# Graph attention and soft expert layer on one core: the order of work in the first stage

## The reference

```python
x = _layernorm(x)
h = (x @ W1.T).reshape(n, 8, 128)
a_src = jnp.einsum('nhc,hc->nh', h, att_src1)
a_dst = jnp.einsum('nhc,hc->nh', h, att_dst1)
e = leaky_relu(a_src[src] + a_dst[dst], 0.2)
ex = jnp.exp(e - segment_max(e, dst)[dst])
alpha = ex / (segment_sum(ex, dst)[dst] + 1e-16)
out = segment_sum(alpha[:, :, None] * h[src], dst) + b1
```

## Time and profile before

| | |
|---|---|
| median of 3 runs | 1894.87 us (1894.81 to 1895.03) |
| the profiled execution: time, span | 1895.43 us, 1893.6 us |
| busy over the span: PE, DVE, ACT, POOL | 91%, 59%, 45%, 14% |
| mean granted TensorE clock | 0.974 |
| products begin, counting begins, counting ends | 31.8 us, 119.3 us, 366.3 us |
| counting: PE's matmuls of edges | 1062, busy 210.1 us |

### The profile page before, as it was taken

One profiled execution on the slowest core, in us unless ns is written; L12 is line 12 of the kernel. 1 busy time (PEld: TensorE's weight loads), 2 busy tenths in 40 slices (PEclk: granted clock), 3 DMA queues, 4 the chain that ended last, 5 costly groups with the idle time before them and its releaser, 6 DMA issues. The chain is left out here.

```text
span 1893.6 us, 30144 instructions
## 1 busy us (share of the span) xinstructions
PE 1720.6 (91%) x9905; PEld 999.8 (53%) x9905; DVE 1118.7 (59%) x1768; ACT 859.8 (45%) x1358; POOL 266.1 (14%) x116
## 2 busy tenths in 40 slices
PE   3988999689999989889997899999999968998899
PEld 2444444366655646545553555556565645665555
DVE  7998777589999936332231355555555555655311
ACT  2257888688888827311111333333333325555200
POOL 1000000178878614000000000000000000000000
PEclk9999999989999989999999999999999988999899
DMA  6000000002222240110000112221111124330421
GB/s 239 23 1 0 29 0 1 0 25 33 35 46 33 21 147 1 55 62 34 34 26 24 62 67 73 71 72 68 65 65 65 65 73 158 111 109 29 151 67 48
DMA packets 49619, 108.41 MB, mean 57 GB/s; under 512 B 16526, under 2 KB 18664, under 8 KB 49420
## 3 DMA queue, kind: packets, MB, share of 16 engines
q1 hardware_dynamic: 49484, 107.38, 18.5%
q10 hardware_dynamic: 64, 0.08, 0.0%
HBM read 79.02 MB, written 28.43 MB: 57 GB/s over the span
## 5 line engine op out<-in xcount | busy, mean ns | idle before, releaser
L829 POOL TENSOR_TENSOR base<-s_row,ln_c 128x1250 f32<-128x1250 f32 x80 | 227.5, 2846 | 56.1 <-DVE top L884 55.2
L728 PE MATMUL fs<-one_src,one_dst 128*128 x1062 | 210.1, 342 | 25.5 <-ACT one_dst L656 14.6
L93 PE MATMUL di_l<-x2t_hi,ph_hi 128*128 128x512 f16 (+1 forms) x576 | 196.3, 341 | 12.4 <-DVE ph_lo L1471 11.0
L94 PE MATMUL di_l<-x2t_lo,ph_hi 128*128 128x512 f16 (+1 forms) x576 | 196.2, 341 | 0.0
L95 PE MATMUL di_l<-x2t_hi,ph_lo 128*128 128x512 f16 (+1 forms) x576 | 196.1, 340 | 0.0
L588 DVE TENSOR_SCALAR one_src<-iota,src 128x1280 f16 x354 | 171.1, 549 | 38.9 <-PE fs L728 32.1
L953 PE MATMUL at_o<-pt,h 128*128 128x384 f32 (+1 forms) x480 | 186.0, 525 | 0.0
L728 PEld LDWEIGHTS fs<-one_src,one_dst 128*128 x1062 | 101.5, 96 | 133.4 <-issue 108.7
L940 PE MATMUL at_t<-ident,q 128*128 128x128 f32 x800 | 108.5, 285 | 29.0 <-ACT q L863 28.2
L93 PE MATMUL co_c<-ps_hi,hid_hi 128*128 128x305 f16 (+1 forms) x384 | 115.3, 300 | 21.2 <-DVE ps_lo L1698 20.6
L940 PEld LDWEIGHTS at_t<-ident,q 128*128 128x128 f32 x800 | 93.1, 146 | 73.8 <-ACT q L863 64.8
(11 more groups left out here) (242 smaller groups left out, 3278.4 us busy)
## 6 DMA issues: line engine op xcount, KB each, us to landing
logits_t<-lg SPq DMA_DIRECT2D x32, 625.0 KB, 3.6
logits_in<-logits_t SPq DMA_DIRECT2D x32, 625.0 KB, 4.1
phf<-in_phi SPq DMA_DIRECT2D x32, 384.0 KB, 3.9
s_row<-a_rows SPq DMA_DIRECT2D x9, 640.0 KB, 5.9
ew1f<-in_fw SPq DMA_DIRECT2D x6, 768.0 KB, 5.1
wf<-in_fw SPq DMA_DIRECT2D x12, 384.0 KB, 6.9
xs<-in_x SPq DMA_DIRECT2D x10, 384.0 KB, 4.0
res<-in_x SPq DMA_DIRECT2D x10, 384.0 KB, 3.0
```

The lines of the kernel that those rows point to most:

```text
L93: eng.matmul(out, lh, rh, start=first, stop=False, skip_group_check=True)
L94: eng.matmul(out, lh, rl, start=False, stop=False, skip_group_check=True)
L728: mm = eng.matmul(counts(j)[:, a:a + n], one_dst[:, ds(slot(pair, m) + i, 1), :], one_src[:, ds(slot(pair, m) + i, 1), a:a + n], start=Fal ...
L829: eng.tensor_tensor(base[:, k % 2, 0:N], s_row[:, head % 2, 0:N], ln_c[:, j, 0:N], ALU.add)\
```

## The change

- DVE starts with the moments and norms of two tiles and the low halves of `W1`. The ranks of edge blocks are cut into pieces, at most one to each turn of the product loop, behind everything else of that turn. `weigh(t-1)` moves ahead of `norm(t+2)`. PE's transposes of `ends` and `top` move behind products 5 and 7.
- SP issues the six slices of `W1` without waiting between them.
- `second_weights(j)` moves out of the product loop to the end of DVE's loop over the edges of tile j, for j from 0 to 7. `W2` is no longer loaded whole: two buffers of one slice each (384 KB), loaded over the halves of `W1` once the products are done. SP issues slices 2 to 7 behind the two `load_s`.
- ACT waits for two free blocks, writes six rows of `apart` and makes one `one_dst` of 768 columns of them. PE waits for `one_dst` once for each pair.
- The three closing matmuls have 2 columns each instead of 512, 512 and 256.

```diff
             for k in range(KD):
-                if k:
-                    eng.wait_ge(in_w1, 16 * k)
-                eng.dma_start(w1f[:, k, :], stored_w1[:, k, :]).then_inc(in_w1, 16)
+                eng.dma_start(w1f[:, k, :], stored_w1[:, k, :]).then_inc(in_w1[k], 16)
...
-            eng.wait_ge(prep, 5)
-            eng.dma_start(attb[:, :, :], att2.unsqueeze(0).to_broadcast([P, 2, D])).then_inc(in_w2[0], 16)
-            eng.dma_start(w2f[:, :, :], w2t.rearrange("(k p) c -> p k c", p=P)).then_inc(in_w2[1], 16)
...
+            def load_w2(k):
+                if k >= 2:
+                    eng.wait_ge(v2_ready, 2 * (k - 1))
+                eng.dma_start(w2f[:, k % 2, :], w2t[k * P:(k + 1) * P, :]).then_inc(in_w2[k % 2], 16)
+
+            eng.wait_ge(h_done, NT)
+            eng.dma_start(attb[:, :, :], att2.unsqueeze(0).to_broadcast([P, 2, D])).then_inc(in_attb, 16)
+            load_w2(0)
+            load_w2(1)
             eng.wait_ge(a_kept, 1)
             eng.dma_start(a_rows, a_turned[:, :]).then_inc(stored, 16)
             eng.wait_ge(stored, 16)
             load_s(0)
             load_s(1)
+            for k in range(2, KC):
+                load_w2(k)
...
-            ranks_of_tiles()
             moments(0)
-            moments(1)
-            nodes_of_edges()
             norm(0)
-            farthest()
+            moments(1)
             norm(1)
-            for k in range(KD):
...
+            low_w1(0)
+            low_x(0)
+            for k in range(1, KD):
+                low_w1(k)
             moments(2)
             for t in range(NT):
                 if t + 1 < NT:
                     low_x(t + 1)
+                if t >= 1:
+                    weigh(t - 1)
                 if t + 2 < NT:
                     norm(t + 2)
                 if t + 3 < NT:
                     moments(t + 3)
-                if t >= 1:
-                    weigh(t - 1)
-                if 1 <= t <= KC:
-                    second_weights(t - 1)
-            eng.wait_ge(v2_ready, 2 * KC)
+                if t == 0:
+                    tiles_of_edges()
+                elif t == 1:
+                    ranks_of_blocks(0, up)
+                elif t == 2:
+                    farthest_ranks(0)
+                elif t == 3:
+                    ranks_of_blocks(1, down)
+                elif t == 4:
+                    farthest_ranks(1)
+                elif t == 5:
+                    nodes_of_edges()
+                elif t == 6:
+                    farthest()
+                elif t == 8:
+                    bounds_of_tiles()
...
-                if j == 1:
+                if j < KC:
+                    second_weights(j)
+                if j == KC:
                     eng.wait_ge(v2_hi, 1)
...
                 with eng.Fori(first, last) as pair:
+                    eng.wait_ge(free, PAIR * pair + PAIR)
                     for n in range(PAIR):
-                        eng.wait_ge(free, PAIR * pair + n + 1)
...
-                        eng.wait_ge(apart_ready, (PAIR * pair + n) * BLOCK + BLOCK)
-                        eng.activation(one_dst[:, ds(slot(pair, n), BLOCK), :], apart[:, n, :, :],
-                                       ACT.Relu, bias=const["one"][:, 0:1], scale=-1.0).then_inc(dst_ready, 1)
+                    eng.wait_ge(apart_ready, (pair + 1) * PAIR * BLOCK)
+                    eng.activation(one_dst[:, ds(slot(pair, 0), PAIR * BLOCK), :], apart[:, ds(pair % 2, 1), :, :],
+                                   ACT.Relu, bias=const["one"][:, 0:1], scale=-1.0).then_inc(dst_ready, 1)
...
                         eng.wait_ge(src_ready, (PAIR * pair + m) * BLOCK + BLOCK)
-                        eng.wait_ge(dst_ready, PAIR * pair + m + 1)
+                        if m == 0:
+                            eng.wait_ge(dst_ready, pair + 1)
...
-                for a, n in CHUNKS_PADDED:
-                    mm = eng.matmul(counts(j)[:, a:a + n], zeros[:, 0:P], zeros[:, 0:n],
+                for a, _ in CHUNKS_PADDED:
+                    mm = eng.matmul(counts(j)[:, a:a + 2], zeros[:, 0:P], zeros[:, 0:2],
                                     start=False, stop=True, skip_group_check=True)
```

More of the change, by code:

```diff
@@ L284, in first_stage @@
     lns = mem("lns", [P, 2, NP], F32)
+    attb = mem("attb", [P, 2, D], F32)
+    w2f = mem("w2f", [P, 2, D], F32)
     assert mem.at <= after_wt
     mem.at = after_wt
[L287 to L290, removed]
     one_src = mem("one_src", [P, BLOCKS * BLOCK, NP], F16)
-    assert mem.at <= after_w2
+    after_one = mem.at
     mem.at = after_wt
@@ L320, in first_stage @@
     one_dst = mem("one_dst", [P, BLOCKS * BLOCK, P], F16)
-    apart = mem("apart", [P, PAIR, BLOCK, P], F16)
+    apart = mem("apart", [P, 2, PAIR * BLOCK, P], F16)
     minus_dst = mem("minus_dst", [P, ETP], F32)
-    in_x, in_w1, in_att, in_w2 = [sem(f"fs_in_x{i}") for i in range(XS)], sem("fs_in_w1"), sem("fs_in_att"), [
-        sem(f"fs_in_w2_{i}") for i in range(2)]
+    in_x, in_w1, in_att, in_attb, in_w2 = (
+        [sem(f"fs_in_x{i}") for i in range(XS)], [sem(f"fs_in_w1_{i}") for i in range(KD)], sem("fs_in_att"),
+        sem("fs_in_attb"), [sem(f"fs_in_w2_{i}") for i in range(2)])
     stats_ready, mean_ready, dev_ready, rstd_ready, normed_ready = (
@@ L433, in ranks_of_tiles, with ranks_of_blocks, farthest_ranks @@
                 eng.wait_ge(iotas, 3)
-                full = [P, NT, ET]
                 eng.tensor_tensor(within[:, :, :], dst_tile[:, :].unsqueeze(1).to_broadcast(full),
                                   tiles[:, :].unsqueeze(2).to_broadcast(full), ALU.is_equal).then_inc(prep, 1)
[L437 to L443, removed]
+            def ranks_of_blocks(n, rank):
+                eng.wait_ge(prep, 2 * n + 1)
+                eng.tensor_tensor(ranks[:, :, :], within[:, :, :],
+                                  rank[:, :].unsqueeze(1).to_broadcast(full), ALU.mult).then_inc(prep, 1)
+            def farthest_ranks(n):
+                eng.wait_ge(prep, 2 * n + 2)
+                eng.tensor_reduce(ends[:, n * NT:(n + 1) * NT], ranks[:, :, :], AX_X, ALU.max).then_inc(prep, 1)
             def nodes_of_edges():
@@ L531, in second_weights @@
                 if k == 0:
-                    for i in range(2):
-                        eng.wait_ge(in_w2[i], 16)
+                    eng.wait_ge(in_attb, 16)
+                eng.wait_ge(in_w2[k % 2], 16 * (k // 2 + 1))
                 for n in range(2):
@@ L536, in second_weights @@
                         eng.wait_ge(v2_ready, 2 * k + n - 1)
-                    eng.tensor_tensor_reduce(unread[:, n, :], w2f[:, k, :], attb[:, n, :], 1.0, 0.0,
+                    eng.tensor_tensor_reduce(unread[:, n, :], w2f[:, k % 2, :], attb[:, n, :], 1.0, 0.0,
                                              ALU.mult, ALU.add, v2f[:, k, n:n + 1]).then_inc(v2_ready, 1)
@@ L551, in finish, with low_w1 @@
                                          ALU.mult, ALU.min).then_inc(out_ready, 1)
-            ranks_of_tiles()
-            moments(0)
-            moments(1)
-            nodes_of_edges()
-            norm(0)
-            farthest()
-            norm(1)
-            for k in range(KD):
+            def low_w1(k):
                 eng.wait_ge(wt_hi, k + 1)
@@ L563, in _ @@
                                          ALU.mult, ALU.subtract).then_inc(wt_lo, 1)
[L564 to L567, removed]
+            moments(0)
+            norm(0)
+            moments(1)
+            norm(1)
+            low_w1(0)
+            low_x(0)
+            for k in range(1, KD):
+                low_w1(k)
             moments(2)
@@ L648, in _ @@
                 with eng.Fori(first, last) as pair:
+                    eng.wait_ge(free, PAIR * pair + PAIR)
                     for n in range(PAIR):
-                        eng.wait_ge(free, PAIR * pair + n + 1)
                         at = block_columns(PAIR * pair + n, shift)
                         for i in range(BLOCK):
-                            eng.activation(apart[:, n, i, :], const["iota"][:, j * P:(j + 1) * P],
+                            eng.activation(apart[:, ds(pair % 2, 1), n * BLOCK + i, :],
+                                           const["iota"][:, j * P:(j + 1) * P],
                                            ACT.Abs, bias=minus_dst[:, ds(at + i, 1)]).then_inc(apart_ready, 1)
-                        eng.wait_ge(apart_ready, (PAIR * pair + n) * BLOCK + BLOCK)
-                        eng.activation(one_dst[:, ds(slot(pair, n), BLOCK), :], apart[:, n, :, :],
-                                       ACT.Relu, bias=const["one"][:, 0:1], scale=-1.0).then_inc(dst_ready, 1)
+                    eng.wait_ge(apart_ready, (pair + 1) * PAIR * BLOCK)
+                    eng.activation(one_dst[:, ds(slot(pair, 0), PAIR * BLOCK), :], apart[:, ds(pair % 2, 1), :, :],
+                                   ACT.Relu, bias=const["one"][:, 0:1], scale=-1.0).then_inc(dst_ready, 1)
                 if j == 0:
```

(10 more changed lines are left out.)

16 lines of the change are left out of this document (6 added, 10 removed).

## The result

The change takes 1897.82 us, median of 20 runs (1895.06 to 1900.26), beside 1894.84 us for the kernel before in as many: a ratio of 1.0018 with a 95% interval of 1.0011 to 1.0025. That is 3 us longer, clear of the noise on this chip, and just inside what the forecast calls no change. It was forecast at 1896.0, in 1890.0 to 1901.5. The profiled execution has a span of 1896.5 us (before 1893.6).

What follows compares the result with a forecast made beforehand. DVE was taken to pace the products and PE the counting. Tile 3 5.5 us late and clock 2.4, less 4.1 for pairs and 3.0 for closings, made +0.8; forecast 1896.0 us, range 1890 to 1901.5.

Steps and rivals of the forecast that it cites:

- Start: DVE's work before the products: ranks leave the front, `x` lands at about 7.9, `low_x(1)` comes at 23.2 instead of 39.6.
- Products: Product loop: pieces lengthen DVE's turns, then PE binds; counting's first matmul at 111.6 instead of 119.33, 7.7 us earlier.
- First pair: Start of the counting: ACT's whole `one_dst` takes 3.1 us against 1.85 before, +1.25 us.
- PE's own issue: Counting: one wait and register instruction fewer save 0.1 for each of 59 pairs, -5.9; narrow closings -3.0.
- the two rivals that took none or all of it: PE's issue between a pair's blocks: doesn't shrink, 1901.9 us, chance 0.22; whole 0.2 goes, 1890.1 us, chance 0.12.
- The closings: End of each counting tile: three 2-column matmuls take 0.18 instead of 0.61, 0.43 a tile, seven counted, -3.0 us.
- Boundary of tiles 0 and 1: Counting: `second_weights(0)` adds 1.8 and ACT's later end 1.2; first matmul of tile 1 at 145.2, before 149.24.
- Boundary of tiles 2 and 3: Counting: DVE waits for slice 2 behind SP's order; PE idles 10.3 us, tile 3 at 204.0, clock +2.4.
- the start did not win less: Rival at the start: first `x` tile or `W1` slice comes 4 us later, 1900 us, chance 0.08.
- slice 2 did not come early: Rival at tiles 2 and 3: SP isn't held, no stall, -10.3 - 2.4, 1883.3 us, chance 0.03.

Runs made afterwards that it cites:

- slices early: The changed kernel with SP issuing slices 2 and 3 of `W2` ahead of its wait for `a_turned`: ratio 0.9945 to the kernel before.
- norm first: The changed kernel with `norm(t+2)` and `moments(t+3)` ahead of `weigh(t-1)` in DVE's turn: ratio 1.0001 to the kernel before, counting begins at 108.43 us.
- ranks first: The changed kernel with the ranks of edge blocks in front of everything again: ratio 1.0028 to the kernel before, counting begins at 117.80 us.
- pairs only: The kernel before with only ACT's pairs (one `one_dst` of 768 columns) and PE's one wait for each: counting takes 246.27 us, before 246.25.
- Closings wide: The changed kernel with closing matmuls of 512, 512 and 256 columns again: ratio 1.0011 to the kernel before, counting takes 259.10 us.

## Why the prediction was right, and where its steps were off

The forecast was no change by cancellation: an earlier counting against one new stall. That is what happened, and slices early shows the stall to be what its step said, SP's order. That the number came within 2 us is in part luck, since one step that failed was partly made up for by others that erred the other way.

1. **Start.** First moments at 7.9, measured 7.77; `low_x(1)` at 23.2, measured 22.97. Right.
2. **Products.** L735 at 111.6, measured 110.91 (112.30 and 112.35 in two other runs with the same order, where the clock fell on the way). That the pieces are on the path and give half of the start back is shown by norm first (2.5 us of it come back when `norm` moves ahead) and ranks first.
3. **First pair.** +1.25, measured 1.2 (3.95 us from L735 for 2.75); six `apart` and one `one_dst` of 768 columns took 1.86 and 0.93. A fall of the clock behind this wait wasn't in the step; it cost nothing in this profile and 0.4 to 1.9 us in eight others.
4. **PE's own issue.** A pair at 3.88, measured 3.89 to 3.91: half of the extra 0.2 it was, and the two rivals that took none or all of it are out. The closings failed. The step took the price of three 2-column matmuls, 0.18, for the time from closing to opening, in the words "Closing a tile took 0.61". They did take little, but the 0.61 is set by the loading of the next tile's bound. 3.0 us of forecast gain were not there, less 0.5 behind the last tile. The trace shows the weight loads of the three narrow closings like this:

```profile
191.93 0.22 PEld L760 LDWEIGHTS fs<-zeros 128*128 128x128 f16 x3
```

The Trainium skill's price of a weight load (TensorE: Matmul & The Clock Gate, section "LDWEIGHTS (loading the stationary operand)"), 107 ns for 128 columns and so 0.32 us for three by the step's estimate, was beside the point as well. In the trace one such load shows 0.10 us, which agrees, but the three overlap to 0.22, and neither figure bounds that gap.
5. **Boundary of tiles 0 and 1.** 145.2, measured 143.28, better than forecast: 0.7 of it was there at L735, and DVE's entry into the loop was counted at before's 1.45 and took 0.38. A fall of the clock after a stall of 4.3 us was not in it; it cost 1.2 us here (8.97 us for two pairs), and it decides whether the pairs of ACT pay at all.
6. **Boundary of tiles 2 and 3.** PE idle 10.3, measured 9.80; tile 3 at 204.0, measured 203.12; clock 2.4, measured 2.0. DVE's own wait was 11.8 us instead of 10: slice 2 took 4.8 us to land, not 4.2, and DVE was through with its loop 1.3 us before ACT began `a_turned` (186.24 and 187.53), where the step had them together. PE's idle time was shorter than forecast all the same, because `a_turned` began at 187.53 and not at 188.4.

The sum: tile 3 late by 4.6, clock 2.0, 41 pairs at 0.09 off, 3.7, closings nothing: +2.9, and 3.0 at the last closing. The forecast's 0.8 misses 2.2 us: the closings 3.0 and the pairs 0.4 to the bad, tile 3 0.9 and the clock 0.4 to the good. (Its own sum gives 1896.2 less 0.6, 1895.6, and not 1896.0.) The miss of *pairs only* has the cause of step 5: the clock was left out, and it took 1.8 us behind the stall of 3.57 us and 0.5 behind the first wait, 2.3 of the 2.9 missing.

The chances on the other side fared so: the start did not win less; slice 2 did not come early.

## What to carry to other kernels

When work moves to another place, follow its loads through the queue that issues them: a load whose buffer was free 52 us earlier stood behind an unrelated wait in SP's order, and 10 us of PE went with it; two lines moved up brought back 12. A stall of the matrix engine costs its length and often some half-speed work behind it. After every stall of 3.57 us or more at the boundaries of tiles in these runs two pairs took 0.25 to 2.0 us more than at full speed; after the wait of 3.20 us this was so in eight traces of eleven, after the 2.50 us of the kernel before in neither of two. So several small delays at one point can be dearer than their sum, and a total that holds such a stall has to be read with the clock beside it. And shortening the last instruction before a gap gains nothing if the gap is made of the next section's register loads: look whether the engine's idle time there says "issue".

## What was not expected of the hardware

- The time from the last matmul of a section to the first of the next didn't depend on those matmuls' columns: 0.58 to 0.65 us with 512, 0.58 to 0.64 with 2 (the boundary with PE's turn of `a_src` left out). Moving the register load behind the opening moved the gap along, 1.14 for 0.67.
- The first entry of DVE into a loop over edges after other code took 1.45, 0.38 and 1.43 us in three programs that differ in what stands before it. Why was not tried.
- At the very start the granted clock reads 1.00 in every trace, though the matmuls of the first product come 0.43 us apart for 1.6 to 4.7 us and 0.215 after. There the pitch tells the clock, not the column. When it rises varies by 2.5 us between programs with the same code up to there (18.8 to 21.4 us), but the start of the counting doesn't follow it. The two traces in which counting begins late, at 112.30 and 112.35 for 110.9 to 111.2, have the clock falling again behind a wait of PE for `normed` of 2.27 us. In three others the same wait of 2.27 us passed without that. Closings wide, just behind it:

```profile
79.00:81.00 2.00, 2.00 (x6) 0.65 (x5) 1.74 (x3) 1.24 (x2) 0.00 (x0) 0.50 0.00 0
```

- The same program's rest took 1528 us on one chip and 1542 to 1550 on others, while before's last closing came at the same time to 0.1 us (365.58 and 365.62).
